# A graph network kernel: one gathered tile in 32 fetched row by row from SyncE and ScalarE

## What is computed

```python
h = relu(layernorm(x)); x = x + layer0   # segment_sum(norm * (h[src] @ W), dst)
h = relu(layernorm(x)); x = x + layer1   # message: MLP(h[src], h[dst], edge features); then a GRU
h = relu(layernorm(x)); x = x + layer2   # GIN: segment_sum(h[src], dst), then an MLP
h = relu(layernorm(x)); x = x + layer3   # SAGE: mean of h[src] by dst, two linear maps, relu
```

## Time and profile before

| | us |
|---|---|
| median of 3 runs | 11380.71 |
| lowest and highest run | 11379.73, 11392.49 |
| the profiled execution's own time | 11306.17 |
| its span in the trace | 11304.4 |

### The profile page before, as it was taken

One profiled execution on the slowest core, in us unless ns is written; L12 is line 12 of the kernel. 1 busy time (PEld: TensorE's weight loads), 2 busy tenths in 40 slices (PEclk: granted clock), 3 DMA queues, 4 the chain that ended last, 5 costly groups with the idle time before them and its releaser, 6 DMA issues. The chain is left out here.

```text
span 11304.4 us, 126194 instructions
## 1 busy us (share of the span) xinstructions
PE 5949.6 (53%) x34165; PEld 5515.0 (49%) x34166; DVE 3267.7 (29%) x4802; ACT 659.7 (6%) x1678; POOL 7460.0 (66%) x6808
## 2 busy tenths in 40 slices
PE   6566656666656777777777333333334333333334
PEld 5555555665656777777777322222223222222224
DVE  9343434334333323222233311111112211111111
ACT  3000000000001000000001000000000000000000
POOL 1888888888875555555654666666665566666665
PEclk6555555555556666666667655555556655555555
DMA  2333333333342111111111111111111111111111
GB/s 71 20 20 20 20 20 20 20 20 20 20 53 52 34 33 34 34 34 34 34 34 24 29 23 23 23 23 23 23 23 20 31 23 23 23 23 23 23 23 29
DMA packets 714529, 310.35 MB, mean 27 GB/s; under 512 B 623117, under 2 KB 627231, under 8 KB 714079
## 3 DMA queue, kind: packets, MB, share of 16 engines
q0 software_dynamic: 398640, 218.14, 16.1%
q1 hardware_dynamic: 314252, 90.77, 3.8%
q10 hardware_dynamic: 1572, 0.67, 0.0%
HBM read 223.75 MB, written 85.30 MB: 27 GB/s over the span
## 5 line engine op out<-in xcount | busy, mean ns | idle before, releaser
L969 POOL DMA_INDIRECT h_rows<-h_tab,idx x3322 | 3159.8, 951 | 1799.7 <-issue 960.3
L1521 PE MATMUL ps_seg<-hot,h_rows 128*64 128x128 f32 x6656 | 1475.9, 413 | 3231.8 <-DVE hot L1406 2979.7
L769 POOL DMA_INDIRECT parts_tab<-total,row_at x1661 | 2559.2, 1541 | 689.1 <-issue 491.2
L1521 PEld LDWEIGHTS ps_seg<-hot,h_rows 128*64 128x64 f32 x6656 | 1321.5, 220 | 3373.5 <-DVE hot L1406 1757.7
L969 POOL DMA_INDIRECT a_rows<-a_tab,idx x1661 | 1579.6, 951 | 1136.7 <-DVE pre L1119 564.7
L1450 DVE TENSOR_TENSOR acc_t<-acc_t,ps_seg 64x128 f32 x416 | 116.4, 280 | 3568.9 <-remote 1386.3
L1141 PE MATMUL ps_seg<-hot,act_rows 128*65 128x128 f32 x3328 | 752.3, 411 | 352.3 <-ACT act_rows L1214 256.7
L1141 PEld LDWEIGHTS ps_seg<-hot,act_rows 128*65 128x65 f32 x3328 | 660.8, 222 | 385.4 <-issue 375.9
L681 PE MATMUL ps_dst<-identb,relb 128*128 128x128 bf16 x1672 | 215.9, 310 | 1075.4 <-DVE relb L615 1075.4
L681 PEld LDWEIGHTS ps_dst<-identb,relb 128*128 128x128 bf16 x1672 | 161.0, 141 | 1111.5 <-DVE relb L615 1107.7
L697 PE MATMUL ps_tot<-msg,same 128*128 128x64 f32 x3328 | 647.8, 376 | 98.4 <-issue 98.4
(11 more groups left out here) (186 smaller groups left out, 5959.4 us busy)
## 6 DMA issues: line engine op xcount, KB each, us to landing
h_rows<-h_tab,idx POOLq DMA_INDIRECT x3322
edge<-edge_t SPq DMA_DIRECT2D x208, 132.0 KB
parts_tab<-total,row_at POOLq DMA_INDIRECT x1661
a_rows<-a_tab,idx POOLq DMA_INDIRECT x1661
parts_tab<-acc_t SPq DMA_DIRECT2D x3, 3360.0 KB
idx<-src_steps SPq DMA_DIRECT2D x624, 4.0 KB
u_win<-u_tab SPq DMA_DIRECT2D x208, 32.0 KB
b_win<-b_tab SPq DMA_DIRECT2D x208, 32.0 KB
```

Of the source, the lines that this page charges most:

```text
L769: pool.indirect_dma_start(parts_tab[:, :], bass.IndirectOffsetOnAxis(ap=row_at[:, b, k:k + 1], axis=0), total[:, b, k, :], None, compute_o ...
L969: pool.indirect_dma_start(dest[:, r, k, :], None, table[:, :], bass.IndirectOffsetOnAxis(ap=idx[:, r, k:k + 1], axis=0)).then_inc(landed[r ...
L1521: last = pe.matmul(ps_seg[0:F, b, 0, :], rows_of[:, r, k, :], hot[:, b, k, :], start=(k == 0), stop=(k == K - 1))
```

## The change

In each turn one tile of the 32 is no longer gathered by GpSimd: tile 0 of the slot r = 3 (`SINGLE_R`, `SINGLE_K`). Its 128 rows are fetched by 128 plain DMAs of 256 bytes, 64 issued by SyncE and 64 by ScalarE. The first stage multiplies the identifiers of these tiles' sources by 256 (one VectorE instruction on 52x128) and stores the byte offsets in `single_tab`. Each of the three edge loops begins with a load of these 6,656 offsets into one partition (`wanted`). To fetch rows an engine loads eight offsets into registers and issues eight DMAs with them.

```diff
+        def single_rows(eng, kind, wanted, table, dest, turn, parts, in_place):
+            flat = table.bitcast(U8).rearrange("(a n) f -> a (n f)", a=1)
+            for first in range(parts.start, parts.stop, SINGLE_GROUP):
+                _, offsets = nc.values_load_multi_w_load_instructions(
+                    wanted[0:1, bass.ds(turn * P + first, SINGLE_GROUP)], engines=[kind], min_val=0,
...
+                for p, offset in enumerate(offsets):
+                    eng.dma_start(dest[first + p:first + p + 1, SINGLE_R, SINGLE_K, :].bitcast(U8),
+                                  flat[0:1, bass.ds(offset, ROW_BYTES)]).then_inc(in_place, 16)
```

In `gather_rows` this tile is skipped, so slot 3 counts seven landings:

```diff
                     for k in range(tiles_of(s)):
+                        if (r, k) in singles:
+                            continue
```

```diff
-                        load_indices(sp, idx, idx_in, landed)
+                        for i in first_loop_last(sp, TURNS):
+                            hold(sp, seg_done, RING * i)
+                            for r in range(RING):
+                                single_rows(sp, mybir.EngineType.SP, wanted, table, rows_of, i, sp_parts[r],
+                                            sp_rows_in[r // 2])
+                                if not (isinstance(i, int) and i == TURNS - 1):
+                                    load_index(i + 1, r)
...
+                                hold(act, seg_done, RING * i)
+                                for h in range(2):
+                                    single_rows(act, mybir.EngineType.Activation, wanted, table, rows_of, i,
+                                                act_parts[h], act_rows_in[h])
...
-                                pe.wait_ge(landed[r], LANDED * i + 16 * tiles_of(s))
+                                if r == SINGLE_R:
+                                    for h in range(2):
+                                        pe.wait_ge(sp_rows_in[h], 512 * i + 512)
+                                        pe.wait_ge(act_rows_in[h], 512 * i + 512)
```

```diff
+                    def turn(i, further_steps):
+                        hold(sp, pre_added, RING * i)
+                        for h in range(2):
+                            single_rows(sp, mybir.EngineType.SP, wanted, a_tab, a_rows, i, sp_parts[h], sp_rows_in[h])
+                        if further_steps:
+                            for r in range(RING):
+                                load_step(i + 1, r)
...
+            act_parts = (slice(64, 88), slice(88, 112), slice(112, P))
...
                     for i in first_then_loop(act, TURNS):
                         for r in range(RING):
+                            if r < len(act_parts):
+                                single_rows(act, mybir.EngineType.Activation, wanted, a_tab, a_rows, i, act_parts[r],
+                                            act_rows_in[r])
+                            rectify(RING * i + r, r % 2)
```

More of the change, by code:

```diff
@@ L11 @@
 I32 = mybir.dt.int32
+U8 = mybir.dt.uint8
 P = 128
@@ L41 @@
 LANDED = 16 * K
+SINGLE_R, SINGLE_K = RING - 1, 0
+SINGLE_GROUP = 8
+ROW_BYTES = 4 * F
 LAST_TILES = -(-N_EDGES // P) - (SUPERS - 1) * K
@@ L959, in load_indices, with gather_rows @@
                                  ).then_inc(idx_in[r], 16)
-        def gather_rows(pool, idx, idx_in, table, dest, landed, used):
+        def single_rows(eng, kind, wanted, table, dest, turn, parts, in_place):
[3 more added lines that the diff above has]
+                    wanted[0:1, bass.ds(turn * P + first, SINGLE_GROUP)], engines=[kind], min_val=0,
+                    max_val=(NP - 1) * ROW_BYTES,
+                    skip_runtime_bounds_check_because="identifiers of nodes are smaller than the table")
+                for p, offset in enumerate(offsets):
+                    eng.dma_start(dest[first + p:first + p + 1, SINGLE_R, SINGLE_K, :].bitcast(U8),
+                                  flat[0:1, bass.ds(offset, ROW_BYTES)]).then_inc(in_place, 16)
+        def gather_rows(pool, idx, idx_in, table, dest, landed, used, singles=()):
             for i in first_loop_last(pool, TURNS):
@@ L1003, in _ @@
                 def _(sp):
-                    for i in first_then_loop(sp, TURNS):
-                        for r in range(RING):
-                            s = RING * i + r
-                            base, more = window_parts_of(s, sp)
-                            hold(sp, landed[r], LANDED * i)
-                            sp.dma_start(idx[:, r, :], src_steps[bass.ds(s, 1), :, :].rearrange("s p k -> p (s k)")
-                                         ).then_inc(idx_in[r], 16)
-                            hold(sp, pre_done, s - RING + 1)
-                            sp.dma_start(edge[:, r, :], edge_t[:, bass.ds(s * ST, ST)]).then_inc(edge_in[r], 16)
-                            sp.dma_start(b_win[:, r, :], b_tab[bass.ds(base, P), :]).then_inc(win_in[r], 16)
-                            with sp.If(more > 0):
-                                seen = before(sp, s)
-                                with sp.Fori(0, more) as w:
-                                    hold(sp, pre_main, s + 1)
-                                    hold(sp, prex_done, seen + w + 1)
-                                    sp.dma_start(b_win[:, r, :],
-                                                 b_tab[bass.ds(further(sp, base, w), P), :]).then_inc(win_x, 16)
-                                    hold(sp, win_x, (seen + w + 1) * 16)
@@ new lines, in load_step @@
+                    def load_step(i, r):
+                        s = RING * i + r
+                        base, more = window_parts_of(s, sp)
+                        hold(sp, landed[r], (LANDED - 16 * (r == SINGLE_R)) * i)
+                        sp.dma_start(idx[:, r, :], src_steps[bass.ds(s, 1), :, :].rearrange("s p k -> p (s k)")
+                                     ).then_inc(idx_in[r], 16)
+                        hold(sp, pre_done, s - RING + 1)
+                        sp.dma_start(edge[:, r, :], edge_t[:, bass.ds(s * ST, ST)]).then_inc(edge_in[r], 16)
+                        sp.dma_start(b_win[:, r, :], b_tab[bass.ds(base, P), :]).then_inc(win_in[r], 16)
+                        with sp.If(more > 0):
+                            seen = before(sp, s)
+                            with sp.Fori(0, more) as w:
+                                hold(sp, pre_main, s + 1)
+                                hold(sp, prex_done, seen + w + 1)
+                                sp.dma_start(b_win[:, r, :],
+                                             b_tab[bass.ds(further(sp, base, w), P), :]).then_inc(win_x, 16)
+                                hold(sp, win_x, (seen + w + 1) * 16)
@@ L1023, in _ @@
+                    sp.dma_start(wanted[:, :], single_tab.rearrange("(a t) p -> a (t p)", a=1)).then_inc(wanted_in, 16)
+                    sp.wait_ge(wanted_in, 16)
+                    for i in first_loop_last(sp, TURNS):
+                        turn(i, not (isinstance(i, int) and i == TURNS - 1))
                 @block.gpsimd
                 def _(pool):
-                    gather_rows(pool, idx, idx_in, a_tab, a_rows, landed, pre_added)
+                    gather_rows(pool, idx, idx_in, a_tab, a_rows, landed, pre_added, ((SINGLE_R, SINGLE_K),))
@@ L1387, in edge_sums @@
                                                  "own_kept"))
+                wanted = sb(ph, f"wanted{layer}", [1, TURNS * P], I32)
+                wanted_in = sem(f"l{layer}_wanted_in")
+                sp_parts = [slice(q * 16, q * 16 + 16) for q in range(4)]
+                act_parts = [slice(64, 96), slice(96, P)]
+                sp_rows_in = [sem(f"l{layer}_sp_rows_in{h}") for h in range(2)]
+                act_rows_in = [sem(f"l{layer}_act_rows_in{h}") for h in range(2)]
                 idx_in = [sem(f"l{layer}_idx_in{r}") for r in range(RING)]
```

62 lines of the change are left out of this document (55 added, 7 removed).

## The result

The changed kernel takes **13,706.1 us** (median of 4 runs, 13,674.7 to 13,719.1) against 11,380.2: a ratio of **1.204, 95% interval 1.201 to 1.206**. The prediction of 11,283 us and its range up to 11,900 were wrong.

What follows compares the result with a forecast made beforehand. Bound: GpSimd and TensorE holding each other in layers two and three, a loop over VectorE, ScalarE and TensorE in layer one. -130 - 30 + 47 + 13 + 3 = -97 us gave 11283 us, range 11180 to 11900.

Steps and rivals of the forecast that it cites:

- The gather saved: Layers two and three: one GpSimd gather of 1.255 us less in each of 104 turns, -130 us.
- The price of a row: SyncE's issue: 0.40 us per row DMA (bounds 0.33 and 0.70), 0.45 us per load of eight offsets.
- 12 us of slack behind SyncE's 31.2 us: Layers two and three: SyncE's 64 rows and loads take 31.2 us; TensorE finishes 12 us after its last handover, hiding them.
- tightest place: Layers two and three: slot 0's indices, now behind 16 rows, make GpSimd wait 0 to 0.2 us.
- Rival one: All layers: rows cost 0.5 to 0.7 us, so slower, 11703 us, or 12288 us at 0.70; chance 0.43.
- Layer one: Layer one's turns: -30 us for the gather saved, +47 us for ReLUs delayed behind ScalarE's rows.
- 5 us of slack: Layer one: next edge features land by 33.5 us, TensorE wants them at 39; used up at 0.49 us a row.
- The ReLUs' delay: Layer one: ScalarE's rows ahead of the ReLUs cost 0.9 us per turn, 47 us, between 0 and 281.
- TensorE's late sums: Layers two and three: sums released only after GpSimd's piece of gathers ends, so a shorter piece should shorten the turn.
- Two queues that issue at once: SyncE and ScalarE issuing together might queue behind one another, one possible reason for rows of 0.5 to 0.7 us.

Runs made afterwards that it cites:

- `only_l23`: The change in layers two and three alone, layer one as in the kernel before: 9860.6 us, ratio 0.987 (quick chip); 12,541.5 us, ratio 1.1005 (slow chip).
- `only_l1`: The change in layer one alone, layers two and three as in the kernel before: 10,179.6 us, ratio 1.019, on a quick chip only.

## Why the prediction was wrong

**The gather saved** (-130 us in layers two and three): right. Skipping the tile shows it on both kinds of chip, and `only_l23` on a quick chip gains it to the microsecond, though the quick chip's turn was not the one the argument described.

**The price of a row** (0.40 us and 0.45 per load of eight offsets on SyncE, so 29.2 us for 64): near outside the slow stretches (27.1 us in `only_l1`, 26.7 in layer one of the changed kernel), and by luck, since two errors cancel. In `only_l1` a row costs 0.32 us and a load of offsets some 0.8, of which 0.69 is the load alone:

```profile
5008.14 2.65 SPq L985 DMA_DIRECT2D a_rows<-a_tab  x8
```

```profile
L980 SPq TENSOR_LOAD <-wanted x416: 690/695/1001, 3457.2 to 5729.8; - x139
```

Inside the slow stretches the price is wrong: the 64 rows take 52.7 us in layers two and three. This is the step that failed. The 0.70 us of the earlier trace rows was taken as the far end of the price of a DMA, when it was the pace of the whole engine in a part of every turn. The register move between two rows pays it too: a row can then cost 0.7 + 0.7 = 1.4 us, outside the bounds that were given.

**12 us of slack behind SyncE's 31.2 us**: wrong with it. At 52.7 us the path passes TensorE's own finish, and rows, landing and handover close a ring that did not exist before. The prediction looked for the damage at slot 0's indices (the "tightest place"). GpSimd does wait there, 5.2 us, but inside the ring, where it costs nothing more.

**Rival one** had the right cause, slow stretches that fall into GpSimd's pieces. The prediction held against it that the decisive rows come before the stretch. It ended at 12,288 us because it charged the indices and ReLUs, not the end of the 64 rows. By its own price of 0.70 these take 64 x 0.70 + 3.6 + 2 = 50.4 us, and with the 1.3 and 4.6 measured behind them a turn of 56 us, close to the 58.6 of the trace. That sum was not made. (The "half of the loads" that it cites are two of the five in the earlier trace rows.)

**Layer one** (-30 + 47 us): wrong on both kinds. "The indices come late for GpSimd as well, but it then works 31 x 1.255 = 39 us in a turn of 52 and waits today" was taken as cover. On a quick chip, where the turn was 39.7 us (`only_l23`, whose layer one is as before: 5543.3 - 3491.2 over 51.75), it is none, and 3.6 us a turn are lost. The step that failed is that SyncE's work of a turn was followed to the edge features only ("5 us of slack") and never added up: it is 44 us, hidden in a turn of 52 but not in one of 39.7. On a slow chip the load of indices stands behind the rows, so GpSimd's run and the rows come one after the other, and the rest of SyncE's work creeps beside the run: +21.7 us a turn, against +0.3 predicted. The ReLUs' delay, for which 47 us were charged, is not on the path: SyncE, which waits for nobody, sets the turn. TensorE waits for ScalarE for 77.7 us in all on the slow chip and 183.9 on the quick one (`only_l1`).

**TensorE's late sums**: the prediction said it would be "wrong altogether if TensorE's late sums grow". They did, to 38 us in layer one (5009.19 to 5047.60), with GpSimd's longer run. The prediction named the 128 DMAs as the cause. But the kernel before has late sums without them, and in those 38 us SyncE issues no row, ScalarE 24. No run tells the two causes apart in layer one. That the release follows the end of GpSimd's piece was read rightly; that a shorter piece is all that follows from it was not.

**Two queues that issue at once.** On a quick chip SyncE issues 64 rows in 27.1 us, 0.42 us each, while ScalarE issues 24 of its own in 10.2 us.
## What to carry to other kernels

An instruction that takes twice its usual time in the trace of before can be a pace, not a price: ask for how long the engine keeps it, and multiply everything you put on that engine there, its register work too. A new chain that gives a slot back only after 64 DMAs is a ring: sum it to its end, at the slow pace, and not only to its first consumer. Add up all that an engine does in a turn, and compare it with the turn. Do not queue another engine's next input behind a long block of issues.

## What the runs showed of the hardware

- **Chips differ by 14% for this kernel.** 9,986 and 9,991 us on two chips, 11,331 to 11,398 in the result's runs and on three others. The same change was worth -1.3% in layers two and three on one kind and +10% on the other. No chip is known to have been used at two times, so chip and time are not told apart.
- On the slow kind, during long unbroken runs of gathers SyncE and ScalarE take about 0.70 us for any instruction, and sums of TensorE are released up to 38 us late. GpSimd's own pitch of 1.255 us is the same on both kinds. Fewer gathers (-1910 us) or a pause every four to eight (-876 us) relieve it; no trace of a quick chip shows it (the longest of 6,656 register moves takes 38 ns there, 1,452 on a slow chip).
- **What it is stays open.** Why chips differ, what is shared between the engines there, and why short pauses leave the kernel before unchanged (46.6 us a turn) was not settled. Every execution behind these numbers was recorded by the profiler, so none tells whether the slow stretches would be there without the recording.
